# Four stacked graph layers on one core: the last normalisation and the squares for the lengths on ScalarE, its bias on GpSimd, and a new order of the steady part

## The chip, the cores and the metric

The kernel runs on one core of one Trainium2 chip. The time is the device time in microseconds (us), lower is better; it is the median of several runs of the same program. TensorE is called PE here, VectorE DVE, ScalarE ACT, GpSimd POOL and SyncE SP, as in the profile.

## The reference

The input is `x` (16 graphs, 1024 nodes, 128 features, f32) and an adjacency `adj` (16 x 1024 x 1024, int32, about 3% ones). Four graph layers follow one another, each with a residual and a layer normalisation:

```python
x = _layernorm(x + _L0_gnn_ref(x, adj, W, a))          # one-head attention, leaky relu scores
x = _layernorm(x + _L1_gnn_ref(x, adj, adj, W, a))     # eight heads, elu
x = _layernorm(x + _L2_gnn_ref(x, adj, ...))           # mean of neighbours, affine norm, relu
x = _layernorm(x + _L3_gnn_ref(x, adj, W))             # four heads of 32
# _L3: Wh = x @ W[h];  scores = Wh Wh^T / sqrt(32);  softmax over neighbours;  attn @ Wh
# _layernorm: (x - mean) / sqrt(var + 1e-5)
```

The softmax of layer 3 is taken with a shift for each head: the largest squared length of a row of `Wh` (by Cauchy-Schwarz no score is above it). So the kernel needs the squares of `Wh`, their sums over 32 columns, and the maximum over all nodes.

## The kernel before

The 16 graphs go through a software pipeline of periods. A period works at the same time on graph n = f+1 (layer 0 and the start of layer 1), graph f (the 64 products of layer 1, as 32 pairs "unit1", and the start of layer 2), graph k = f-1 (layer 2 and layer 3: 32 score tiles of 128 x 1024 whose exponentials ACT makes) and graph m = f-2 (the end of layer 3: turned back, divided, residual, normalised, stored). The nodes lie in T = 8 tiles of 128 partitions.

For each engine a table (`ON_PE`, `ON_ACT`, `ON_DVE`, `ON_POOL`, `ON_SP`) gives each job its place in the order of the engine's instructions; the number is only a rank within the engine and no time. Engines meet only through semaphores. Stage 3 of the tables is the steady part, used for 13 periods (f = 2 to 14); stages 0 to 2 are the start and stage 4 is the end (f = 15, 16, 17).

Layer 3 of graph k runs so: DVE writes `x3` (`layer2_norm`, job "norm3"); PE turns it (`layer3_turn`, L825); ACT copies it to `xbT`; PE multiplies with the weights in both directions (`layer3_project`: L1020 with the nodes on partitions, then L1026 with the features on partitions); ACT copies the first result to `w3` (`layer3_project` on ACT, signal `w3_ready`) and the second to `shared` (`layer3_wide`, `wT_ready`); SP copies halves of it across partitions (`spread_far`, L713, "far"). DVE squares `w3` (L1700), sums (L1702), takes the maximum (L1704); PE and DVE spread it over the partitions (L1031, L1709, L1711, L1035, L1716), which gives `shift_ready`. The first scores (L1056, L1063, job "scores3" 0) wait for the copy across, for the shift and for `mask3_made`. That mask is a GpSimd transfer that adds -1 to the adjacency tile (L778). Other GpSimd transfers are the next adjacency (L792) and the residual added to `x4` (L784, "residual3"); all three are in one queue.

The last normalisation of graph m: DVE makes the statistics (job "stats3", L1395 to L1407), POOL the power -1/2 (`rstd_tail`, L757, into row 5 of `tsmall`), and DVE eight instructions `(x4 + row 0) * row 5`, one for each node tile (`layer3_normalise`, job "tail3", L1412, tile `elu`, of which `x4` is another name). SP then stores (`store_out`, L718). The squares go into `squares3`, another name of `yb`.

```python
def rstd(var_ready, rstd_ready, small, b, n):
    pool.wait_ge(var_ready.sem, var_ready.of(b, n + 1))
    pool.tensor_tensor(small[:, 5, :], small[:, 4, :], half_neg[:], ALU.pow).then_inc(rstd_ready.sem, 1)
```

Of the kernel before, what the change touches and what calls it, by code (L numbers as in the profile page):

```python
# [22 lines left out]
ALU = mybir.AluOpType  # L23
# [49 lines left out]
def graph_stack(nc, x, adj, L0_gnn_W, L0_gnn_a, L1_gnn_W, L1_gnn_a, L2_gnn_rel_weights, L2_gnn_self_w,  # L73
                L2_gnn_self_b, L2_gnn_ln_gamma, L2_gnn_ln_beta, L3_gnn_W, out):
    NB, N, D = x.shape
    T = N // P
# [46 lines left out]
    with ExitStack() as ctx:  # L123
# [282 lines left out]
        trstd_ready = signal("trstd_ready", 1)  # L406
        x3_ready = signal("x3_ready", 1)
# [37 lines left out]
        def schedule(tables, step):  # L445
# [3 lines left out]
            for stage, periods in zip(STAGE, SECTIONS):  # L449
                for s in range(STEPS):  # L450
# [30 lines left out]
            (dict(maxima1=92, maxima3=43, project0=[28, 29, 34], project1=90, project2=102, project3=41, scores3=[49,  # L481
                 53, 56, 58, 65, 70, 75, 82, 84, 86, 89, 93, 96, 100, 103, 105], self2=0, self_weights=-1, shift3=47,
                 sources1=94, spread0=48, spread1=97, sum1=[19, 24, 25, 26, 35, 36, 37, 38], sum2=[1, 2, 3, 6, 9, 12,
                 16, 17], top0=44, turn0=[10, 20], turn1=88, turn2=98, turn3=39, turn_back=32, unit0=[72, 73, 74, 77,
                 78, 79, 80, 81], unit1=[4, 5, 7, 8, 11, 13, 14, 15, 18, 21, 22, 23, 27, 30, 31, 33, 40, 42, 45, 46,
                 50, 51, 52, 55, 59, 60, 61, 62, 66, 67, 68, 69], values3=[54, 57, 63, 64, 71, 76, 83, 85, 87, 91, 95,
                 99, 101, 104, 106, 107]),),
            (dict(maxima1=-1, maxima3=42, project0=[-1, -1, -1], project1=-1, project2=73, project3=39, scores3=[45,
                 47, 53, 58, 61, 63, 65, 66, 69, 72, 76, 79, 83, 90, 92, 93], self2=0, self_weights=-1, shift3=44,
                 sources1=-1, spread0=-1, spread1=-1, sum1=[16, 19, 24, 25, 28, 31, 32, 34], sum2=[1, 2, 3, 4, 8, 10,  # L490
                 13, 15], top0=-1, turn0=[-1, -1], turn1=-1, turn2=71, turn3=35, turn_back=18, unit0=[-1, -1, -1, -1,
                 -1, -1, -1, -1], unit1=[5, 6, 7, 9, 11, 12, 14, 17, 20, 21, 22, 23, 26, 27, 29, 30, 33, 36, 37, 38,
                 40, 41, 43, 46, 48, 50, 51, 52, 55, 56, 57, 59], values3=[49, 54, 60, 62, 64, 67, 68, 70, 74, 75, 84,
# [253 lines left out]
        def _(pool):  # L747
# [1123 lines left out]
```

## Time and profile before

| | us |
|---|---|
| median of 3 runs (2472.6 to 2477.9) | 2477.36 |
| profiled execution, its own time | 2477.37 |
| span of its trace | 2475.3 |
| busy: PE, DVE, ACT, POOL | 2232.8, 2226.2, 1939.2, 227.8 |

The profiled execution is one run of the program; about 2 us of its time lie outside the span. Busy time leaves out waits; matmuls are pipelined and their ends are modelled. The steady part is most of the run: the mask transfer of L778 is issued once in a period, and from one issue to the next pass about 145 us.

### The profile page before, as it was taken

Reading aid. Unit: us, or ns where it says so; the run is one execution under the profiler, and the core shown is the slowest. Engines: PE = TensorE matmul, PEld = TensorE weight load, DVE = VectorE, ACT = ScalarE, POOL = GpSimd, SP = SyncE. Lnnn points to the kernel's source line nnn. Section 1 sums busy time; section 2 is a strip of 40 time slices with the busy share of each in tenths; the row PEclk is TensorE's granted clock in tenths of the full one; section 3 lists DMA queues with packets and bytes.
Section 4 is the critical chain, followed back from the end, with each engine's and each line's share of the span. In section 5 each row is a group of like instructions: output and inputs, shape, how many; then the busy total and the mean of one; then the engine's idle time right before and its main releaser. Section 6 shows DMA issues by size and latency. Waiting matters only on the chain.

```text
span 2475.3 us, 56568 instructions
## 1 busy us (share of the span) xinstructions
PE 2232.8 (90%) x23539; PEld 1506.0 (61%) x23629; DVE 2226.2 (90%) x4195; ACT 1939.2 (78%) x2152; POOL 227.8 (9%) x135
## 2 busy tenths in 40 slices
PE   4678999999999999999999999999999999998876
PEld 3567566575756657585665757566575765657431
DVE  3898899999999999999999999999999999999766
ACT  2758798787889878787987879798787978877634
POOL 0001010010101001010010101001010100101010
PEclk9889999999999999999999999999999999999988
DMA  6238034452614445251544526144352624504000
GB/s 132 89 93 162 11 98 84 111 96 70 112 50 123 86 104 103 70 112 44 129 86 96 111 52 126 48 121 95 84 123 44 127 54 121 95 27 85 19 18 17
DMA packets 258799, 212.10 MB, mean 86 GB/s; under 512 B 137648, under 2 KB 235056, under 8 KB 257584
## 3 DMA queue, kind: packets, MB, share of 16 engines
q1 hardware_dynamic: 191424, 135.61, 19.5%
q0 software_dynamic: 67120, 72.88, 19.2%
q8 instruction: 186, 3.05, 0.5%
q14 instruction: 69, 0.57, 0.1%
HBM read 151.78 MB, written 42.53 MB: 79 GB/s over the span
## 4 chain that ended last, share of the span: by engine, by line
PE 57%; DVE 22%; issue 10%; ACT 6%; DMA 3%; POOL 0%; SPq 0%; POOLq 0%; DVEq 0%; ACTq 0%
PE kp L1080 14%; PE kp L1063 10%; PE fp L883 9%; DVE weight L1586 8%; PE fp L954 7%; PE kp L1056 4%; ACT weight L1305 3%; DMA shared<-shared 2%; DVE bstat L1395 2%; PE kp L1004 2%; PE kp L935 2%; DVE yb L1412 2%; PE fp L832 1%; DVE yb L1662 1%; PE fp L972 1%
## 5 line engine op out<-in xcount | busy, mean ns | idle before, releaser
L1257 ACT ACTIVATE ramp<-s1row,tbig 128x1024 bf16<-128x1024 f32 x854 | 913.0, 1147 | 32.1 <-DVE weight L1586 31.1
L1305 ACT ACTIVATE weight<-kp,shift 128x1024 f32<-128x1024 f32 x480 | 510.8, 1110 | 206.7 <-PE kp L1063 190.4
L1586 DVE TENSOR_TENSOR weight<-ramp,AT 128x2048 bf16<-128x2048 bf16 x512 | 609.4, 1220 | 41.8 <-PE fp L954 30.9
L1080 PE MATMUL kp<-weight,w 128*33 128x512 f32 x1920 | 457.6, 600 | 15.7 <-DVE weight L1726 7.3
L954 PEld LDWEIGHTS fp<-vh_parts,weight 128*128 128x128 bf16 x8192 | 391.9, 98 | 100.3 <-DVE weight L1586 52.0
L954 PE MATMUL fp<-vh_parts,weight 128*128 128x102 bf16 x8192 | 425.5, 209 | 29.5 <-DVE weight L1586 22.6
L1726 DVE SCALAR_TENSOR_TENSOR weight<-AT,weight 128x1024 f32<-128x1024 bf16 x272 | 321.6, 1219 | 34.7 <-ACT weight L1305 34.4
L1063 PE MATMUL kp<-shared 32*128 32x512 f32 x1920 | 274.5, 641 | 16.3 <-ACT weight L1305 16.2
L1080 PEld LDWEIGHTS kp<-weight,w 128*33 128x33 f32 x1920 | 94.2, 110 | 310.3 <-issue 225.2
L883 PEld LDWEIGHTS fp<-features,weight 128*128 128x128 f32 x1920 | 218.8, 193 | 38.1 <-issue 37.3
L883 PE MATMUL fp<-features,weight 128*128 128x129 f32 x1920 | 224.2, 278 | 13.3 <-DVE weight L1496 12.6
L935 PE MATMUL kp<-vh_parts,AT 128*128 128x136 bf16 x3072 | 219.1, 232 | 1.6 <-ACT vh_rest L1173 1.1
L935 PEld LDWEIGHTS kp<-vh_parts,AT 128*128 128x128 bf16 x3072 | 211.8, 100 | 2.5 <-ACT vh_rest L1173 1.3
L1205 ACT ACTIVATE weight<-xfT,v0neg,v0s 128x1024 f32<-128x1024 f32 x128 | 155.4, 1245 | 46.7 <-PE fp L883 44.3
L1496 DVE SCALAR_TENSOR_TENSOR weight<-weight,v,AT 128x1024 f32<-128x1024 f32 x128 | 158.9, 1281 | 15.8 <-ACT weight L1205 12.1
L1004 PE MATMUL kp<-elu,AT 128*128 128x128 bf16 x1920 | 170.2, 220 | 0.0
L1001 PE MATMUL kp<-y_hi,AT 128*128 128x129 bf16 x960 | 166.2, 221 | 3.0 <-DVE elu L1646 3.0
L1063 PEld LDWEIGHTS kp<-shared 32*128 32x128 f32 x1920 | 76.1, 183 | 128.3 <-issue 67.9
L757 POOL TENSOR_TENSOR bsmall<-bsmall,half_neg 128x8 f32<-128x8 f32 x32 | 68.2, 2130 | 895.2 <-DVE bsmall L1407 895.2
L1004 PEld LDWEIGHTS kp<-elu,AT 128*128 128x128 bf16 x1920 | 148.7, 98 | 0.2
L1056 PE MATMUL kp<-AT,big 128*128 128x512 bf16 x390 | 107.5, 382 | 35.7 <-DMA shared<-shared 20.8
L1594 DVE TENSOR_REDUCE vh<-fp 128x272 f32<-128x816 f32 x128 | 128.1, 1001 | 6.2 <-PE fp L954 6.1
(222 smaller groups left out, 2690.4 us busy)
## 6 DMA issues: line engine op xcount, KB each, us to landing
s1row<-s_rows_dram SPq DMA_DIRECT2D x128, 512.0 KB, 4.3
adj_bf_dram<-in_adj_dram POOLq DMA_DIRECT2D x15, 2048.0 KB, 12.8
AT<-minus POOLq DMA_DIRECT2D x15, 2048.0 KB, 18.2
x<-in_x_dram SPq DMA_DIRECT2D x16, 512.0 KB, 5.0
xfT<-s_row_dram SPq DMA_DIRECT2D x16, 512.0 KB, 4.3
out_dram<-elu SPq DMA_DIRECT2D x16, 512.0 KB, 3.2
shared<-shared SPq DMA_DIRECT2D x30, 256.0 KB, 3.6
elu<-x POOLq DMA_DIRECT2D x15, 512.0 KB, 5.2
```

Of the source, the lines that this page charges most:

```text
L883: last = pe.matmul(sums0(b)[:, g, n * (D + 1):(n + 1) * (D + 1)], ring0(b)[:, jt % P0_RING, t * P:(t + 1) * P], h0[:, jt, :], start=(jt == ...
L935: last = pe.matmul(kp[:, SUM_A_BANKS[t // PER], n * H1 * C1:(n + 1) * H1 * C1].rearrange("p (h c) -> p h c", h=H1), AT[:, third, jt, t * P ...
L954: last = pe.matmul(fp[:, 1 + t // 4, col:col + 2 * PARTS * C1], edges[:, u % B_RING, t * P:(t + 1) * P], vh_parts[:, jt, h, :, :, :].rearr ...
L1001: pe.matmul(sums2(b)[:, g, col:col + D + 1], lhsT, y2_hi[:, jt, :], start=(jt == 0), stop=False, skip_group_check=True)
L1004: last = pe.matmul(sums2(b)[:, g, col:col + D], lhsT, low2(b)[:, jt, k, :], start=False, stop=(jt == T - 1 and k == 1), skip_group_check=True)
L1056: pe.matmul(score_banks(b, w)[:, x, :], big[:], AT[:, third, 2 * J + x, n * HALF:(n + 1) * HALF], start=True, stop=False, skip_group_check ...
L1063: last = pe.matmul(score_banks(b, w)[:, x, :], mine[:, jt * P:(jt + 1) * P], mine[:, n * HALF:(n + 1) * HALF], start=v in masks(b), stop=True,
L1080: last = pe.matmul(kp[side(h), 0, :], values3(b)[:, (2 * J + x) * H3 + h, :], weight3[:, w % P_RING, x * HALF:(x + 1) * HALF], start=(J == ...
L1257: act.activation(ramp[:, u % R_RING, :], s1row[:, h % S_RING, :], ACT.Relu, bias=tbig1[:, jt, h:h + 1], scale=BIG).then_inc(ramp_ready, 1)
L1305: act.activation(weight3[:, w % P_RING, :], score_banks(b, w).rearrange("p a n -> p (a n)"), ACT.Exp, bias=shifts3(b)[:, h:h + 1], scale=R ...
L1586: dve.tensor_tensor(edges[:, u % B_RING:u % B_RING + 2, :], ramp[:, u % R_RING:u % R_RING + 2, :], AT[:, third, jt:jt + 2, :], ALU.min).th ...
L1726: dve.scalar_tensor_tensor(out=mine, in0=AT[:, third, 2 * J:2 * J + 2, n * HALF:(n + 1) * HALF], scalar=1.0 if b < NB - 1 else 0.0, in1=mi ...
```

## The change

1. `layer3_normalise` moves from DVE to ACT: eight ACTIVATEs of 128 x 128 with function Identity, bias and scale each a column of `tsmall` (rows 6 and 5).
2. POOL's `rstd_tail` also multiplies row 0 (minus the mean) by row 5 into row 6 and signals `tshift_ready`, for which ACT waits.
3. The squares move from DVE to ACT: after the copy to `w3` ACT reads the same PSUM tile once more with function Square and writes `squares3`; only then comes `w3_ready`. DVE's L1700 and one wait go.
4. The tables of stages 3 and 4 have a new order on all five engines.

```diff
             def rstd_tail(b):
                 rstd(tvar_ready, trstd_ready, tsmall, b, 0)
+                pool.wait_ge(trstd_ready.sem, trstd_ready.of(b))
+                pool.tensor_tensor(tsmall[:, 6, :], tsmall[:, 0, :], tsmall[:, 5, :], ALU.mult) \
+                    .then_inc(tshift_ready.sem, 1)
...
             def layer3_project(b):
                 act.wait_ge(w3_made.sem, w3_made.of(b))
                 src = projected3(b).rearrange("p a (b o) -> p (a b) o", o=O3)
-                copy(values3(b)[:, :, 0:O3], src).then_inc(w3_ready.sem, 1)
+                copy(values3(b)[:, :, 0:O3], src)
+                act.activation(squares3, src, ACT.Square).then_inc(w3_ready.sem, 1)
...
+            def layer3_normalise(b):
+                act.wait_ge(tshift_ready.sem, tshift_ready.of(b))
+                for t in range(T):
+                    last = act.activation(x4[:, t, :], x4[:, t, :], ACT.Identity, bias=tsmall[:, 6, t:t + 1],
+                                          scale=tsmall[:, 5, t:t + 1])
+                last.then_inc(x4_ready.sem, 1)
...
-                dve.tensor_tensor(squares3, values3(b)[:, :, 0:O3], values3(b)[:, :, 0:O3], ALU.mult).then_inc(back.sem, 1)
-                dve.wait_ge(back.sem, back.step())
                 dve.tensor_reduce(q3[:], squares3, AX_X, ALU.add).then_inc(back.sem, 1)
...
-            def layer3_normalise(b):
-                dve.wait_ge(trstd_ready.sem, trstd_ready.of(b))
-                normalise(x4, x4, tsmall, x4_ready.sem)
...
         ON_POOL = [
...
-            (dict(adjacency=6, mask3=1, residual3=3, rstd0=5, rstd1=7, rstd2=0, rstd3=2, rstd_tail=4),),
+            (dict(adjacency=1, mask3=0, residual3=4, rstd0=6, rstd1=7, rstd2=2, rstd3=3, rstd_tail=5),),
```

The tables for the steady part, read as orders around the jobs that matter here (before, then after):

```
PE   turn3 etc.:  turn_back unit1[15] project0[2] sum1[4..7] turn3 unit1[16] project3 unit1[17] maxima3 top0 unit1[18] unit1[19] shift3 spread0 scores3[0]
                  project0[2] turn_back sum1[4..7] unit1[15] turn3 unit1[16] top0 project3 unit1[17] maxima3 unit1[18] unit1[19] shift3 spread0 scores3[0]
PE   first jobs:  self2 sum2[0..2] unit1[0] unit1[1]      |  sum2[0..2] self2 unit1[0] unit1[1]
DVE  middle:      out2 unit1[11] stats2 head1[2] unit1[12..14] affine2 unit1[15] relu2 unit1[16] finish3 norm3 head1[3] ... top0 unit1[19] lengths3
                  out2 unit1[11..12] stats2 head1[2] unit1[13..14] affine2 relu2 unit1[15] top0 unit1[16] norm3 finish3 head1[3] ... unit1[19] most0 lengths3
DVE  last jobs:   cut1[1] masked3[14] rest2 low2 cut1_third[0]  |  cut1[0] rest2 cut1[1] masked3[14] cut1_third[0] low2
ACT:              unit0[0..2] exp3[10] exp3[11] unit0[3..5]     |  unit0[0..2] tail3 exp3[10] exp3[11] unit0[3..5]
ACT:              exp3[22] sources1 exp3[23]                    |  exp3[22] exp3[23] sources1
POOL:             rstd2 mask3 rstd3 residual3 rstd_tail rstd0 adjacency rstd1
                  mask3 adjacency rstd2 rstd3 residual3 rstd_tail rstd0 rstd1
SP:               adjacency x ... far store_row sources[3] spread_row sources[4]
                  x adjacency ... far sources[3] sources[4] store_row spread_row
```

In stage 4, "tail3" of graph 14 was on DVE between `masked3[13]` and `masked3[14]` of graph 15; it is now on ACT behind its last exponential. "tail3" of graph 15 is the last job on DVE before, and the last on ACT after.

## Rows read from the trace of the kernel before

**Rows 1.** Busy time by engine in one steady period and in two stretches of it.

```profile
1236.00:1382.00 146.00, 138.55 (x1482) 94.09 (x1486) 137.20 (x260) 121.79 (x136) 14.57 (x9) 0.99 0.43 92
...
1217.30:1263.50 46.20, 42.91 (x652) 40.60 (x649) 45.58 (x97) 37.89 (x45) 8.34 (x4) 0.96 0.56 93
1268.00:1354.00 86.00, 83.91 (x657) 42.98 (x662) 78.78 (x147) 70.10 (x79) 5.95 (x4) 1.00 0.26 65
```

**Rows 2.** GpSimd in order of time: first and last mask issue, twelve intervals apart.

```profile
366.55 3.21 POOL L778 DMA_DIRECT2D AT<-minus  x1
...
2109.16 3.22 POOL L778 DMA_DIRECT2D AT<-minus  x1
```

**Rows 3.** Chain that ended last, in order of time, one period: start, us, what.

```profile
1217.29 0.06 DVE weight L1586
...
1267.71 0.81 PE kp L1056 x3
```

**Rows 4.** Groups of instructions by form: what leaves DVE, and GpSimd's power.

```profile
L1412 DVE TENSOR_SCALAR elu<-elu,tsmall 128x128 f32<-128x128 f32 x128 | 34.2, 341 | 1.8 <-POOL tsmall L757 1.8
L1700 DVE TENSOR_TENSOR yb<-w 128x1024 f32<-128x1024 f32 x15 | 18.3, 1223 | 2.1 <-ACT w L1173 2.1
L757 POOL TENSOR_TENSOR tsmall<-tsmall,half_neg 128x8 f32<-128x8 f32 x16 | 33.3, 2083 | 323.4 <-DVE tsmall L1407 323.4
```

**Rows 5.** Groups by form on ScalarE: copies, two column operands, the table load.

```profile
L1205 ACT ACTIVATE weight<-xfT,v0neg,v0s 128x1024 f32<-128x1024 f32 x128 | 155.4, 1245 | 46.7 <-PE fp L883 44.3 <-PE kp L883 2.3
L1173 ACT ACTIVATE features<-fp 128x384 f32<-128x384 f32 x64 | 30.0, 505 | 0.0
L1173 ACT ACTIVATE w<-kp 128x1024 f32<-128x1024 f32 x15 | 15.4, 1026 | 26.6 <-PE kp L1020 26.6
L1173 ACT ACT_TABLE_LOAD x1 | 1.3, 1283 | 0.8 <-PEq L1860 0.8
```

**Rows 6.** TensorE in order of time in one period; brackets: idle before, releaser.

```profile
1209.36 0.61 PE L982 MATMUL kp<-bias_parts,part_rows 65*128 65x512 bf16 x2
...
1233.58 0.90 PE L954 MATMUL fp<-vh_parts,weight 128*128 128x102 bf16 x16 [0.41 <-DVE weight L1586]
...
1246.37 1.22 PE L954 MATMUL fp<-vh_parts,weight 128*128 128x102 bf16 x16 [0.35 <-DVE weight L1586]
...
1263.52 0.27 PE L1031 MATMUL kp<-ident,qmax 128*4 128x128 f32 x1 [1.44 <-DVE qmax L1704]
...
1267.71 0.81 PE L1056 MATMUL kp<-AT,big 128*128 128x512 bf16 x3 [2.05 <-DVE vh L1594]
...
1302.56 1.14 PE L1063 MATMUL kp<-shared 32*128 32x512 f32 x8
...
1336.61 1.14 PE L1063 MATMUL kp<-shared 32*128 32x512 f32 x8 [0.43 <-ACT weight L1305]
```

**Rows 7.** VectorE, then ScalarE, in order of time, same period.

```profile
1208.44 1.23 DVE L1646 TENSOR_TENSOR elu<-yf,elu 128x1024 bf16<-128x1024 f32 x1 [2.02 <-ACT elu L1173]
```

```profile
1261.40 1.02 ACT L1173 ACTIVATE shared<-kp 128x1024 f32<-128x1024 f32 x1 [0.69 <-PE kp L1026]
...
1297.63 2.11 ACT L1305 ACTIVATE weight<-kp,shift 128x1024 f32<-128x1024 f32 x2
...
1316.70 2.12 ACT L1305 ACTIVATE weight<-kp,shift 128x1024 f32<-128x1024 f32 x2 [6.11 <-PE kp L1063]
```

**Rows 8.** First scores (L1056) of two other periods: the wait for the copy across.

```profile
1122.05 0.81 PE L1056 MATMUL kp<-AT,big 128*128 128x512 bf16 x3 [3.08 <-DMA shared<-shared]
...
1412.39 0.81 PE L1056 MATMUL kp<-AT,big 128*128 128x512 bf16 x3 [1.17 <-DMA shared<-shared]
```

**Rows 9.** The end of the run: ScalarE, then VectorE.

```profile
2392.68 1.02 ACT L1173 ACTIVATE s1row<-fp 128x1024 f32<-128x1024 f32 x1 [0.73 <-PE fp L1026]
```

```profile
2304.93 2.12 DVE L1412 TENSOR_SCALAR elu<-elu,tsmall 128x128 f32<-128x128 f32 x8
...
2469.51 2.14 DVE L1412 TENSOR_SCALAR elu<-elu,tsmall 128x128 f32<-128x128 f32 x8 [1.75 <-POOL tsmall L757]
```

More of the change, by code:

```diff
@@ new lines, in graph_stack @@
+                 tail3=-1, turn0=[9, 14], turn1=70, turn2=82, turn3=21, unit0=[50, 51, 52, 56, 57, 58, 60, 61],
+                 wide3=27),),
+            (dict(cut1=[84, 86], cut1_second=[90, 91], elu=63, exp3=[31, 32, 34, 35, 38, 39, 41, 42, 46, 47, 54, 55,
+                 59, 60, 64, 65, 66, 67, 69, 70, 72, 73, 75, 76, 78, 79, 83, 85, 88, 89, 92, 93], exps0=36, exps1=80,
+                 first2=87, out3=[49, 68, 81, 97], prepare0=48, project0=[16, 17, 20], project1=74, project3=26,
+                 ramps=[0, 1, -1, 2, 3, 4, -1, 5, 6, 8, 9, 10, 11, 14, 18, 19, 21, 22, 28, -1, 29, 30, -1, 33, 37, -1,
+                 40, 43, 44, 45], ramps_ahead=[95, 96], second2=94, self2=7, sources1=77, sum1=[15, 23, 25], tail3=53,
+                 turn0=[12, 13], turn1=71, turn2=82, turn3=24, unit0=[50, 51, 52, 56, 57, 58, 61, 62], wide3=27),),
@@ L615, in graph_stack @@
             (dict(adjacency=3, mask3=0, residual3=-1, rstd0=4, rstd1=5, rstd2=1, rstd3=2, rstd_tail=-1),),
[L616 to L617 removed]
+            (dict(adjacency=1, mask3=0, residual3=4, rstd0=6, rstd1=7, rstd2=2, rstd3=3, rstd_tail=5),),
+            (dict(adjacency=-1, mask3=0, residual3=3, rstd0=-1, rstd1=5, rstd2=1, rstd3=2, rstd_tail=4),
                  dict(adjacency=-1, mask3=-1, residual3=8, rstd0=-1, rstd1=-1, rstd2=6, rstd3=7, rstd_tail=9),
@@ L627, in graph_stack @@
                  store_row=8, store_sources=10, x=0),),
-            (dict(adjacency=0, far=5, out=10, sources=[2, 3, 4, 7, 9], sources_ahead=[12, 13, 14], spread_row=8,
-                 store_row=6, store_sources=11, x=1),),
-            (dict(adjacency=-1, far=4, out=6, sources=[0, 1, 2, 3, 5], sources_ahead=[-1, -1, -1], spread_row=-1,
+            (dict(adjacency=1, far=5, out=10, sources=[2, 3, 4, 6, 7], sources_ahead=[12, 13, 14], spread_row=9,
+                 store_row=8, store_sources=11, x=0),),
+            (dict(adjacency=-1, far=5, out=6, sources=[0, 1, 2, 3, 4], sources_ahead=[-1, -1, -1], spread_row=-1,
                  store_row=-1, store_sources=-1, x=-1), dict(adjacency=-1, far=7, out=8, sources=[-1, -1, -1, -1, -1],
@@ L1342, in step @@
                         layer3_out(k, g)
+                if m is not None and s == at["tail3"]:
+                    layer3_normalise(m)
                 for w in range(U3):
@@ L1802, in step @@
                     layer2_norm(k)
-                if m is not None and s == at["tail3"]:
-                    layer3_normalise(m)
                 if k is not None and s == at["lengths3"]:
```

165 lines of the change are left out of this document (80 added, 85 removed).

## The prediction

> **What bounds the kernel now.** I read first the busy time by stretches [rows 1]. In a steady window of 146.0 us PE works 138.55 and DVE 137.20: both are at 94 to 95%, ACT is at 121.79, POOL at 14.57. So two engines are nearly full, and the question is which one is full where. The mask transfer tells the length of a period: (2109.16 - 366.55) / 12 = 145.2 us [rows 2]. Thirteen periods of it are 1888 us, three quarters of the run.
>
> The chain of waits then tells the place [rows 3]: from about 1217.3 it runs through DVE, up to 1267.71, where the first scores begin; from there it lies on PE for the rest of the period. The two stretches in [rows 1] say the same in busy time: in 46.2 us DVE works 45.58 and PE 42.91, in the following 86.0 us PE works 83.91 and DVE only 78.78. The reader is to see that a microsecond taken from DVE can only pay in the first third of the period, and that even there PE follows closely: it has 46.2 - 42.91 = 3.3 us to give.
>
> Where PE's gaps are, its own order of time shows [rows 6]: 0.41 and 0.35 us behind DVE's pairs, 1.44 us for the maximum of the lengths, 2.05 us before the first scores, later 0.43 us for an exponential. The gap before the first scores is put down to a DVE reduction in this period; in the two other periods shown it ended with the copy across (3.08 and 1.17 us) [rows 8]. The gaps of 1.44 and 2.05 us are not work but the latency of a chain: x3 turned, copied, projected, copied, sent across. Less DVE work doesn't shorten that.
>
> **What leaves DVE.** Eight normalising instructions and one square for each graph: 34.2 / 16 = 2.14 us and 1.22 us [rows 4], together 3.36 us in a period of 145.2. Over the run that is 54 us of busy time, and it is the most that this part could bring.
>
> **What comes to ACT.** The square reads the same PSUM tile as the copy to `w3`, 128 x 1024: 1.03 us by that copy, of which about 0.1 us overlaps the one before it [rows 5]. No ACTIVATE of 128 x 128 stands in the trace. The copies of 384 and 1024 columns (0.505 and 1.026 us) give 0.81 ns a column; the form with two column operands takes 1.245 us at 1024, so at 128 it is an estimated 1.245 - 896 x 0.00081 = 0.52 us [rows 5]. Eight of them cost 4.2 us with no overlap; if the two column operands cost nothing, 8 x (0.505 - 256 x 0.00081) = 2.4 us. Between these I take 3.3 us, near the row with the same operands, less 0.1 us of overlap for each. So ACT gets 4.2 us for the 3.36 us that DVE loses, and rises to 126 of 145. It's not the bound by sum, only by place.
>
> The Trainium skill, page "ScalarE: Activation LUTs", section "What ACT_TABLE_LOAD costs", gives 186 ns + 0.833 ns a column, 93 ns more for each column operand and 93 ns of overlap. By that the eight would be an estimated 3.2 us; the sum would be the same. The same page ("Rules for kernel authors") says to keep multiplications and additions on VectorE. In this trace the group on DVE takes 0.34 us each, against my 0.52 us, so the rule agrees with the rows on the price, and speaks against this change wherever ACT is the one that's awaited.
>
> **Place by place in the steady period.** All times are those of the period in [rows 6, 7].
>
> 1. Square before the wide copy. ACT's copy to `w3` would end at about 1260.7, the square at 1261.7, and the wide copy began at 1261.40, when PE had finished its input [rows 7]. It begins 0.2 to 0.3 us later, and so does everything on the copy across, which is what the first scores wait for: +0.2 us. The bounds are 0 and 1.0 us (the whole square in the way). The maximum of the lengths comes earlier, because 1.22 us on DVE are replaced by 0.9 on ACT, and because DVE has less to do; but that is not the last wait here, so it pays nothing.
>
> 2. Order between the layer-2 output and `x3`. DVE now writes `x3` before it finishes graph m, and pair 15 comes behind relu. `x3` can be some 1.2 us earlier. But PE turns it only after pair 15 and the eight sums, and that work is unchanged. It gains what it waited for: 0.35 us at 1246.37, since pair 15 is now long ready, and some of the 0.41 us at 1233.58, if DVE comes to the output of layer 2 a little ahead: I take 0.3. Sum -0.65 us.
>
> 3. Start of the period. PE took the bias product at 1209.36, with the sums of layer 2 behind it; now those sums are first. They need the lowest part, which DVE wrote from 1208.44 to 1209.67 behind ACT's copy [rows 6, 7]. DVE fills its 2.02 us of waiting with another job, but the part isn't ready sooner. PE waits about 0.3 us there: +0.3.
>
> 4. The normalisation on ACT. It stands before exponentials 10 and 11, which began at 1297.63 and ended near 1299.7 [rows 7]. With 3.3 us ahead of them they end at 1303.0. PE needs them for the scores at 1302.56 [rows 6]: it waits 0.4 us. Behind that ACT had 6.11 us of idle time before 1316.70 [rows 7], so the delay doesn't travel. Bounds: 0 us (the eight in 2.4 us end at 1302.1) and 1.3 us (4.2 us). POOL's multiplication (not in the trace; below the 2.1 us of its power [rows 4]) is hidden: the statistics are made tens of microseconds before ACT comes there.
>
> 5. Exponentials 22 and 23 are now neighbours; the row copy stood between them, and PE waited 0.43 us at 1336.61 [rows 6]. -0.4 us.
>
> 6. GpSimd's queue. The mask is issued ahead of the power, as soon as the sums of layer 2 are there, and the next adjacency right behind it. Both are awaited late: the mask by the first scores, the adjacency in the next period. The power for layer 2 now stands behind two issues (3.2 us for the mask [rows 2]), but DVE asks for it only after the output and the statistics, eight instructions each and a pair between, the output's alone at about the 0.34 us of such an instruction [rows 4], 2.7 us; a delay of the power would be 0.5 us at most. On SP x goes ahead of the turned adjacency, and the row's store behind two loads of sources; what they feed is behind several pairs. Zero, with rival C for the price if the cover fails.
>
> Sum: +0.2 - 0.65 + 0.3 + 0.4 - 0.4 = -0.15 us in a period, -2.0 us in thirteen.
>
> **The end.** For graph 15 ACT is idle and nothing hides a latency. PE's second half of the wide product waits for `w3_ready` in the last graph, and so ACT's copy of it at 2392.68 [rows 9] comes a square later: +1.0 us. The final normalisation was 2.14 us on DVE, the last work before the store [rows 9]; it becomes 3.3 us on ACT, behind one more POOL instruction: +1.2, and 0.1 to 2.1 us for the multiplication (a whole power as the upper bound [rows 4]), of which I take 0.3. In period 15, where PE isn't full, DVE's 2.12 us of normalising at 2304.93 [rows 9] and the square go from a chain that DVE often bounds; I take half of 3.4 us: -1.7. The end's sum is +0.8 us.
>
> Together -1.2 us, against the profiled execution's 2477.37 us; the median of the runs is 2477.36, so no correction is needed. Small gains that I can't place (DVE relieved by 3.36 us a period, with an order made for it) are more probable than small losses: I say 2475.5 us. A difference under 0.2%, 5 us, is about what a measurement of this kernel can't tell from none.
>
> **Rivals.**
>
> A, DVE's relief is worth more. For it speaks that DVE is full in the first stretch [rows 1, 3]; if PE's 0.41 and 0.35 us go and another 0.4 us of the latency chain, because `x3` is earlier and PE gets to it earlier, a period loses about 0.9 us: 13 x 0.9 = 12 us, 2466. PE's whole 3.3 us of gaps in that stretch is the limit: 13 x 3.3 = 43 us, 2434, which needs the latency to vanish. Against it: the gaps [rows 6, 8] show that most of the gap is not DVE's.
>
> B, ACT is in the way, the other side. If the square delays the copy across by its full 1.0 us and the normalisation holds PE by its upper bound of 1.3 us, less the 0.7 us of points 2, 3 and 5, a period grows by 1.6 us; with a part of it, 0.9 us, the end is 13 x 0.9 + 2 = 14 us later: 2491. It decides from the point where the eight ACTIVATEs take more than about 4 us. For it: ACT's idle time comes in one piece behind that place, 6.11 us before 1316.70 [rows 7], and not ahead of it.
>
> C, the transfers meet after all. The adjacency, 2 MB, now runs behind the mask into the time when residual and copy across go. Then the copy across lands late, as in the period with 3.08 us against the one with 1.17 [rows 8]: 1.9 us each, 13 x 1.9 = 25 us, 2500. For it: these rows. Against: the mask itself, which runs ahead of both, now starts earlier, since nothing of DVE's stands before it.
>
> D, Square isn't in the loaded table. The trace has one load, 1.28 us, for all functions used so far [rows 5]. Two loads a graph, before the wide copy and after it, put at least 2.6 us on ACT and 1.3 us on the chain: 16 x 1.3 = 21 us or more, 2498.
>
> **Chances.** My forecast, within 0.2%: 0.39. A, faster by over 0.2%: 0.38, with sizes spread from 2440 to 2472. B 0.14, C 0.06, D 0.03, together 0.23 slower. The range must leave out 2 in 10: the far part of A below 2461, and C, D and the far part of B above 2489. My forecast's own range is 2472 to 2482.
>
> **What would show it.** Right: DVE's busy time down by about 54 us, ACT's up by 60 to 70, PE's unchanged; a period of 144.8 to 145.4 us by the mask issues; PE's gap at the first scores still about 3 us in sum with the one for the maximum, and ended by the copy across; a gap near 0.4 us behind the normalisation on ACT; one table load. Wrong: a DVE group of the same sum as before; a gap at the first scores of 4 us or more (B, C); Identity instructions of 0.3 us, with no gap behind them (A).

## The result, and the profile after

The changed kernel takes 2509.96 us in the median (2507.65 to 2515.18, 4 runs), the kernel before on the same chip 2474.98 us (2472.39 to 2477.90, 4 runs): 1.0145 times the time before, 95% interval 1.0126 to 1.0164. The prediction was 2475.5 us with a range up to 2489; the forecast missed the sign and is 34.5 us off, 21 us of it beyond the end of the range.

The page of the changed kernel: busy time by engine, the chain that ended last, the group of the first scores, and two transfers with their time to landing (the last column).

```profile
span 2513.4 us, 56584 instructions
PE 2245.2 (89%) x23539; PEld 1504.7 (60%) x23629; DVE 2173.9 (86%) x4051; ACT 1996.9 (79%) x2296; POOL 245.6 (10%) x151
...
PE 55%; ACT 21%; issue 10%; DVE 9%; DMA 4%; SPq 0%; POOL 0%; ACTq 0%; DVEq 0%; POOLq 0%
...
L1063 PE MATMUL kp<-AT,big 128*128 128x512 bf16 x390 | 111.0, 394 | 51.3 <-DMA shared<-shared 40.7
...
adj_bf_dram<-in_adj_dram POOLq DMA_DIRECT2D x15, 2048.0 KB, 29.2
AT<-minus POOLq DMA_DIRECT2D x15, 2048.0 KB, 19.8
```

The same chain and the same group in the kernel before:

```profile
PE 57%; DVE 22%; issue 10%; ACT 6%; DMA 3%; POOL 0%; SPq 0%; POOLq 0%; DVEq 0%; ACTq 0%
...
L1056 PE MATMUL kp<-AT,big 128*128 128x512 bf16 x390 | 107.5, 382 | 35.7 <-DMA shared<-shared 20.8
```

What was moved has moved as intended: DVE is down by 52.3 us to 2173.9 (54 were expected) and ACT up by 57.7 to 1996.9 (60 to 70). But in the chain that ended last ACT has taken DVE's place: ACT has 21% and DVE 9%, where DVE had 22% and ACT 6%. The group with the first scores, L1063, waits 40.7 us in the run for the copy across, 20.8 us before.

In the kernel after, the groups by form that answer to [rows 4, 5]: the normalisation, the square, the table load.

```profile
L1319 ACT ACTIVATE elu<-elu,tsmall 128x128 f32<-128x128 f32 x128 | 51.0, 492 | 10.2 <-POOL tsmall L778 10.2
L1298 ACT ACTIVATE yb<-kp 128x1024 f32<-128x1024 f32 x15 | 15.3, 1018 | 0.0
L1180 ACT ACT_TABLE_LOAD x1 | 1.3, 1283 | 0.8 <-PEq L1869 0.8
```

These prices are as predicted: 0.492 us for one of the eight (0.52), 1.02 us for the square, one table load. Rival D falls. The 35 us are not in the price of an instruction.

GpSimd's mask issues, first and thirteenth, as in [rows 2]:

```profile
363.92 3.22 POOL L785 DMA_DIRECT2D AT<-minus  x1 [44.26 <-PE kp L1011]
...
2138.23 3.23 POOL L785 DMA_DIRECT2D AT<-minus  x1 [43.14 <-PE kp L1011]
```

(2138.23 - 363.92) / 12 = 147.86 us a period against 145.2: +2.64 us. The first scores of the first and the thirteenth steady period, before and then after, tell where the 38.1 us between the two spans (2513.4 - 2475.3) lie:

```profile
396.04 0.81 PE L1056 MATMUL kp<-AT,big 128*128 128x512 bf16 x3 [1.58 <-DMA shared<-shared]
...
2138.28 0.81 PE L1056 MATMUL kp<-AT,big 128*128 128x512 bf16 x3 [1.19 <-DMA shared<-shared]
```

```profile
402.26 0.81 PE L1063 MATMUL kp<-AT,big 128*128 128x512 bf16 x3 [2.27 <-DMA shared<-shared]
...
2176.37 1.37 PE L1063 MATMUL kp<-AT,big 128*128 128x512 bf16 x3 [2.27 <-DMA shared<-shared]
```

Up to the first of them the changed kernel has lost 6.2 us, in the twelve periods between them 31.9 us, and from there to the end of the span nothing: 337.0 us in both. For the start I had put nothing, for the end +0.8 us.

Windows over the stretches that answer to [rows 1], and over the first 3.7 us behind the first scores. Columns: stretch, its length, busy time and instructions of PE, its weight loads, DVE, ACT, POOL; granted clock; DMA share; GB/s.

```profile
1257.00:1403.00 146.00, 137.75 (x1449) 92.30 (x1453) 130.60 (x236) 122.50 (x142) 14.79 (x9) 0.98 0.39 88
1386.00:1432.10 46.10, 42.22 (x659) 39.58 (x657) 44.37 (x98) 37.85 (x45) 8.94 (x5) 1.00 0.76 138
1436.30:1440.00 3.70, 3.69 (x22) 1.31 (x22) 3.16 (x7) 1.43 (x3) 0.00 (x0) 0.61 0.54 192
```

The last row is what no row of the kernel before shows in this place: PE works all the time and was granted 0.61 of its clock, most of the stretch at 1.2 instead of 2.4 GHz. PE in order of time around it, the part that answers to [rows 6]:

```profile
1405.47 0.66 PE L851 MATMUL fp<-ident,x 128*128 128x128 f32 x4 [1.09 <-ACT xfT L1180]
...
1426.28 2.02 PE L1027 MATMUL kp<-rhs,xbT 128*128 128x128 f32 x16 [0.41 <-ACT vh_rest L1180]
...
1431.83 0.27 PE L1038 MATMUL kp<-ident,qmax 128*4 128x128 f32 x1 [1.08 <-DVE qmax L1719]
1431.93 1.60 PE L961 MATMUL fp<-vh_parts,weight 128*128 128x102 bf16 x32
1433.47 0.27 PE L1042 MATMUL kp<-qdiag,ones 4*128 4x4 f32 x1
...
1436.31 1.48 PE L1063 MATMUL kp<-AT,big 128*128 128x512 bf16 x3 [2.46 <-DMA shared<-shared]
1437.73 1.84 PE L1070 MATMUL kp<-shared 32*128 32x512 f32 x8
```

The three matmuls of L1063 take 1.48 us here and 0.81 in the kernel before, the eight behind them 1.84 and 1.14. In 9 of the 13 steady periods the granted clock falls like this at the scores, and the stage from the first scores to the first unit of layer 0 takes 30.7 to 31.8 us instead of 29.3. Two more periods of the changed kernel: in the first the copy across was late as well, in the second the clock stayed:

```profile
697.86 0.84 PE L1063 MATMUL kp<-AT,big 128*128 128x512 bf16 x3 [4.22 <-DMA shared<-shared]
698.63 2.09 PE L1070 MATMUL kp<-shared 32*128 32x512 f32 x8
...
993.18 0.81 PE L1063 MATMUL kp<-AT,big 128*128 128x512 bf16 x3 [2.26 <-DMA shared<-shared]
993.92 1.14 PE L1070 MATMUL kp<-shared 32*128 32x512 f32 x8
```

Read the brackets ahead of the scores with those of before. There, PE waited 1.44 us for the maximum of the lengths and 2.05 ahead of the scores [rows 6]. In six of its 13 steady periods the two waits are 1.78 and about 1.2 us [rows 8 has one of the second], in the other seven 1.43 and 1.55 to 3.08. Now the first is 1.08 in every period and the second 2.26 to 2.5 us in eight of 13, 2.67 to 4.22 in the five in which the copy across is late. Where no copy is late, the sum is 3.3 to 3.6 us against 2.9 to 3.1; the second wait has become the long one. Its length alone doesn't decide: the kernel before kept its clock behind 2.05, 2.29 and 3.08 us [rows 6, 8 have two of them], this one behind 2.26 or 2.27 us in three periods and behind 3.63 in one.

Where the period grew, in means over eleven periods of each kernel, the second to the twelfth steady one, worked out from PE's and DVE's order of time. The stages run from the reading of layer 2's sums to the turn of layer 3, its projection, the first scores, the first unit of layer 0, the projection of layer 1 that follows layer 0 (the recorded expectations call this point the layer-0 turn), and the next reading. "Half clock" counts periods in which the stage behind the scores is longer than 30.2 us.

| kernel | to turn 3 | to projection | to scores | to unit 0 | to layer 1 | to next | period | half clock |
|---|---|---|---|---|---|---|---|---|
| before | 25.67 | 2.18 | 9.86 | 29.33 | 30.98 | 47.20 | 145.23 | 0 of 11 |
| after | 25.95 | 2.58 | 10.50 | 30.52 | 31.35 | 47.11 | 148.01 | 8 of 11 |
| squares alone (e7) | 25.82 | 2.15 | 10.45 | 30.99 | 30.98 | 47.19 | 147.59 | 10 of 11 |
| squares, filled wait (e16) | 25.68 | 2.17 | 9.98 | 29.59 | 30.99 | 47.20 | 145.62 | 0 of 11 |
| normalisation alone (e8) | 25.71 | 2.17 | 9.78 | 29.36 | 31.39 | 47.19 | 145.60 | 0 of 11 |
| after, filled wait (e5) | 26.42 | 2.56 | 9.92 | 29.33 | 31.35 | 47.11 | 146.70 | 0 of 11 |
| before, filled wait (e15) | 25.68 | 2.17 | 9.56 | 29.56 | 30.99 | 47.21 | 145.17 | 0 of 11 |
| before, joined waits (e18) | 25.79 | 2.16 | 9.62 | 31.08 | 30.99 | 47.20 | 146.83 | 9 of 11 |

One caution: the first scores begin with four matmuls of 128 x 512. The traces of e15, e16 and e18 hold all four records, the others in the table only three (0.81 us, where four take 1.02). So in these three rows "to scores" is about 0.2 us too short against the others and "to unit 0" as much too long; between the two groups only the sum of these two stages can be compared. Where a record is missing, the wait in the bracket before it is too long by the same 0.2 us. It is 39.2 us before, 41.0 after, 39.1 in e15, 39.6 in e16 and 40.7 in e18.

### The profile page after: what moved, and what is told of

It reads as the page before. It is cut to its first block, busy times and chain, and to the rows that moved or that the text cites. A ratio compares the mean times of both kernels' runs of the same rounds, so it can differ in the third digit from the quotient of the medians.

```text
span 2513.4 us, 56584 instructions
## 1 busy us (share of the span) xinstructions
PE 2245.2 (89%) x23539; PEld 1504.7 (60%) x23629; DVE 2173.9 (86%) x4051; ACT 1996.9 (79%) x2296; POOL 245.6 (10%) x151
## 4 chain that ended last, share of the span: by engine, by line
PE 55%; ACT 21%; issue 10%; DVE 9%; DMA 4%; SPq 0%; POOL 0%; ACTq 0%; DVEq 0%; POOLq 0%
PE kp L1087 12%; PE kp L1070 11%; ACT ramp L1264 9%; PE fp L961 7%; PE fp L890 6%; ACT weight L1313 5%; PE kp L942 5%; PE kp L1063 4%; DVE weight L1603 4%; DMA shared<-shared 3%; ACT elu L1319 2%; PE fp L839 2%; PE fp L979 1%; PE kp L1104 1%; ACT shared L1180 1%
## 5 line engine op out<-in xcount | busy, mean ns | idle before, releaser
L961 PEld LDWEIGHTS fp<-vh_parts,weight 128*128 128x128 bf16 x8192 | 393.2, 98 | 115.9 <-issue 69.9
L961 PE MATMUL fp<-vh_parts,weight 128*128 128x102 bf16 x8192 | 424.5, 210 | 30.7 <-DVE weight L1603 15.2
L1070 PE MATMUL kp<-shared 32*128 32x512 f32 x1920 | 282.6, 658 | 17.1 <-ACT weight L1313 15.9
L942 PEld LDWEIGHTS kp<-vh_parts,AT 128*128 128x128 bf16 x3072 | 205.6, 98 | 0.7
L1063 PE MATMUL kp<-AT,big 128*128 128x512 bf16 x390 | 111.0, 394 | 51.3 <-DMA shared<-shared 40.7
L1589 DVE TENSOR_SCALAR ramp<-s1row,st 128x1024 bf16<-128x1024 f32 x170 | 120.2, 749 | 11.8 <-DMA s1row<-s_rows_dram 10.8
## 6 DMA issues: line engine op xcount, KB each, us to landing
adj_bf_dram<-in_adj_dram POOLq DMA_DIRECT2D x15, 2048.0 KB, 29.2
```

Of the source, the lines that this page charges most:

```text
L942: last = pe.matmul(kp[:, SUM_A_BANKS[t // PER], n * H1 * C1:(n + 1) * H1 * C1].rearrange("p (h c) -> p h c", h=H1), AT[:, third, jt, t * P ...
L961: last = pe.matmul(fp[:, 1 + t // 4, col:col + 2 * PARTS * C1], edges[:, u % B_RING, t * P:(t + 1) * P], vh_parts[:, jt, h, :, :, :].rearr ...
L1063: pe.matmul(score_banks(b, w)[:, x, :], big[:], AT[:, third, 2 * J + x, n * HALF:(n + 1) * HALF], start=True, stop=False, skip_group_check ...
L1070: last = pe.matmul(score_banks(b, w)[:, x, :], mine[:, jt * P:(jt + 1) * P], mine[:, n * HALF:(n + 1) * HALF], start=v in masks(b), stop=True,
```

## The experiments

Ratios are to the kernel before on the same chip. "Old order" means the order tables of the kernel before.

### Order or work: e1 to e4

e1: all that was moved, in the old order (ACT normalises behind the third unit of layer 0). e2: the kernel before with the new orders of PE, ACT, DVE, POOL and SP, nothing moved. e3: the changed kernel with the old orders of POOL and SP. e4: the changed kernel with two entries of ACT exchanged:

```
-  ... sum1[1], turn3, sum1[2], project3 ...
+  ... sum1[1], sum1[2], turn3, project3 ...
```

> All three edits of the change (normalisation and square on ACT, bias on POOL), but the orders of the kernel before; the normalisation stands behind layer-0 tile 2 on ACT, as in the changed kernel. If the new order is the cause, this is near before: 2475 plus 13 x 0.6 us (square 0.2, normalisation 0.4) plus 2 us at the end, about 2485, ratio 1.004 (range 1.000 to 1.007), steady period 145.2 to 146. If the moved work itself is the cause, it is near the changed kernel: 2510, ratio 1.014.

2514.43 us, 1.0155 (1.0140 to 1.0170). The moved work is enough by itself for a loss of this size; the new order isn't needed for it.

> The kernel before with the new orders alone; normalisation and square stay on DVE, the normalisation at its old place in the order of DVE. If the order is the cause: slower than before by 25 us or more, ratio 1.010 or above, period 147 us or more. If the moved work is the cause: within 5 us of before. An order made for a relieved DVE may do worse with the full one: up to 3.4 us a period more, 2550.

2495.35 us, 1.0078 (1.0061 to 1.0095). The new order costs with the old work, too: with DVE's work undiminished it takes 40.2 us from the projection to unit 0 instead of 39.2, and no period loses the clock at the scores.

> The changed kernel with the orders of POOL and SP of the kernel before. If the transfers that now lie close together cost the late copies across (four of twelve periods 1.2 to 1.9 us late) and the wait for row loads: 10 to 15 us less than the changed kernel, 2497, ratio 1.009. If transfers are innocent: 2510, ratio 1.014, and the half clock falls as often.

2525.01 us, 1.0202 (1.0186 to 1.0217): the new orders of GpSimd and SyncE save the changed kernel 15 us; without them the stage to turn 3 is 26.70 us instead of 25.95. Rival C named the wrong suspect: with GpSimd's old order four of the 13 copies across still land 10.7 to 11.3 us behind the projection, where a copy in time takes 9.1 to 9.4. The adjacency's 29.2 us to landing cost nothing that a run shows.

> The changed kernel with one swap on ACT in the steady part: the third sum's copy comes ahead of the copy of x3, as before. The projection no longer waits for it: 0.4 us less before the first scores in each of 13 periods, 5 us, 2505. If the shorter gap also keeps the clock up in the periods where it fell (1.5 us each, nine periods): 12 to 18 us less, 2495, ratio 1.008. If the gap simply moves to the copy across: 2510.

2506.22 us, 1.0125 (1.0110 to 1.0140), 3.7 us less, with intervals that overlap. The wait of 0.41 us at the projection is gone in the trace (2.20 instead of 2.58 us for the stage).

### Which of the two moves: e7 and e8

e7 is the kernel before with the first edit below, e8 with the second (in the old order, ACT normalises behind the third unit of layer 0).

```
 # e7: layer3_project on ACT
-                copy(values3(b)[:, :, 0:O3], src).then_inc(w3_ready.sem, 1)
+                copy(values3(b)[:, :, 0:O3], src)
+                act.activation(squares3, src, ACT.Square).then_inc(w3_ready.sem, 1)
 # and the tensor_tensor of layer3_lengths on DVE is gone
 # e8: layer3_normalise on ACT, the product of rstd_tail on POOL, as in the change
```

> The kernel before with one thing of the change: the squares by ScalarE ahead of the wide copy, no product on VectorE. Order and normalisation as before. Theory 'square': taking the product off VectorE brings the lengths' wait on PE forward and so makes of two short waits one longer one in front of the first scores, and the clock falls there: most of the old-order kernel's +38 us is already here, time 2500 to 2515. Rival 'normalisation': the square costs 0.2 us a period, 2478 to 2482, and the clock keeps its 0.97 to 0.98.

2502.92 us, 1.0105 (1.0080 to 1.0130). PE in e7, the first scores in two periods with the same wait:

```profile
546.40 1.46 PE L1056 MATMUL kp<-AT,big 128*128 128x512 bf16 x3 [2.04 <-DVE vh L1595]
...
2169.49 0.81 PE L1056 MATMUL kp<-AT,big 128*128 128x512 bf16 x3 [2.04 <-DVE vh L1595]
```

The clock was lost in the first and kept in the second; e7 loses it in 11 of 13 steady periods, also behind 1.97 us, where the kernel before kept it behind 2.05.

> The kernel before with the other half: the last normalisation as eight ACTIVATEs on ScalarE behind the third copy of the shared layer-0 turn (and the bias product on GpSimd), the product of squares still on VectorE, order otherwise as before. Theory 'square': the clock is kept, the eight cost PE 0.3 to 0.4 us a period in waits for exps and VectorE has 2.4 us more room: 2476 to 2485. Rival 'normalisation': the exps and copies of the layers behind it slip and the clock falls from that: 2500 to 2515 here.

2482.85 us, 1.0033 (1.0016 to 1.0050). The squares, the smaller of the two moves (1.2 us of DVE's time), cost 27 us; the normalisation costs 7. Together 34, while both at once in the same order cost 38 (e1) and the whole change 35. The table says where: with the squares alone 10 of 11 periods lose the clock, with the normalisation alone none, and there only the stage with the eight ACTIVATEs has grown, by 0.41 us.

### The wait ahead of the scores: e5, e6, e16, e15, e18

e5 puts matmuls of no use into PE's wait for the copy across; their product goes to a part of PSUM that nobody reads. e16 is the same on e7, e15 with eight of them on the kernel before.

```
 def layer3_spread_maxima(b):
     ...
+    if b < NB - 1:
+        for _ in range(16):
+            pe.matmul(kp[:, 4, HALF // 2:HALF], big[:], minus[:], start=True, stop=True, ...)
```

> The changed kernel with sixteen matmuls of no use (256 columns each, about 1.7 us in all) put on PE right behind the transposed maxima, in the wait for the copy across; the output doesn't change. Theory 'clock': in nine of twelve periods of the changed kernel the granted clock falls to half at the first scores, right behind PE's longest wait, and these scores and the 1.5 us around them then cost 1.4 to 1.6 us more. With PE busy in that wait the clock stays up: first scores to the first unit0 back at 29.4 us in nearly all periods, mean granted clock above 0.98, time 2496 (2490 to 2502), 12 to 20 us below the changed kernel. Rival 'ScalarE in the way': the clock only mirrors waits that cost anyway; the time stays at 2510 (2506 to 2514), whatever the clock does. Rival 'late transfer' (the copy across lands late): also unchanged, or up by at most 1 us a period if the matmuls outlast the wait.

2494.25 us, 1.0078 (1.0054 to 1.0102): 15.7 us less than the changed kernel, for work of no use. PE in order of time in e5:

```profile
1419.50 1.92 PE L1046 MATMUL kp<-minus,big 128*128 128x256 bf16 x16
1421.35 0.38 PE L872 MATMUL fp<-tmost,ones 1*128 1x1 f32 x2
1421.89 0.81 PE L1067 MATMUL kp<-AT,big 128*128 128x512 bf16 x3 [0.16 <-issue]
1422.63 1.14 PE L1074 MATMUL kp<-shared 32*128 32x512 f32 x8
```

The scores are back at 0.81 and 1.14 us, in every period, and only one of the 13 copies across is late, by 0.35 us, against five in the changed kernel. Part of the gain is lost again: the half clock now falls ahead of the turn of layer 3 in 5 of 13 periods instead of 1 (26.42 us to turn 3 instead of 25.95). The page "TensorE: Matmul & The Clock Gate" of the Trainium skill, section "HAM oscillation — how this bites in real kernels", says that a wait for a transfer between groups of matmuls can take the clock away so that the next group starts at half speed. The trace agrees, with 1.48 against 0.81 us, and here a wait of 2.3 to 2.5 us with only short matmuls ahead of it was enough in most periods.

e6 moves the square behind the wide copy in all graphs but the last.

> The changed kernel with the Square behind the wide copy instead of ahead of it, in all graphs but the last. Theory 'clock': the copy across is issued about 1.0 us earlier, but the lengths come that much later, so the wait before the transposed maxima grows and the one before the scores shrinks by as much; the clock is kept in more periods if the length of the single wait decides. Time 2500 to 2510. If only the 0.2 to 0.4 us that the Square puts ahead of the copy matter: 2507 (2504 to 2510). If the lengths set the end of that chain: the wait moves on and the time stays within 2 us of 2510.

2500.34 us, 1.0099 (1.0076 to 1.0122). The long wait is now the one for the maximum (2.81 us), the one ahead of the scores only 0.56; the scores run at full clock in all periods, but in every second one the half clock falls into the short work between the two waits (the 32 matmuls of L961 take 2.82 us instead of 1.60), and the scores come 1.3 to 1.4 us later. That is 60% of e5's gain, by moving the wait and not filling it; about 0.1 us a period of it comes from the copy across, which is issued 4.83 instead of 4.94 us behind the projection.

> Control: the kernel before with eight matmuls of no use (about 1.0 us) in the same wait. No clock is lost at its first scores, so by the theory there is nothing to win: 2476 (2473 to 2479). If such matmuls help in another way (a warmer engine later on), it becomes faster by 5 us or more, and the repair of the changed kernel proves less than I took from it.

2473.80 us, 0.9983 (0.9973 to 0.9992). Not the nothing that I expected, but 4 us and not 16: the steady part gives almost nothing (39.1 instead of 39.2 us from the projection to unit 0, a period of 145.17 instead of 145.23). Of the 5.5 us between the two profiled executions 1.5 lie ahead of the first unit 0 of the steady part and 3.6 behind the last one; why is open.

> The kernel with the squares alone on ScalarE (2503, 27.5 us over the kernel before) with the sixteen matmuls in PE's wait. Theory 'clock': the scores run at the full clock again (first scores to unit0 29.33 us in all periods) and the late copies across go as they did in the changed kernel: 2479 (2476 to 2484). Rival: if 10 us or more of the 27.5 stay, the moved squares cost something besides: 2488 or more.

2482.11 us, 1.0020 (1.0011 to 1.0029): of the squares' loss 21 us are gone (1.0105 to 1.0020). What is left is 0.4 us a period. Against e15, which has a filler and no moved square, 0.42 us more lie in the stage to the scores; 0.13 of it are late copies (two against one), so at most about 0.3 is left for the square ahead of the wide copy, which was priced at 0.2; e16's filler is also the longer one.

e18 is the converse: the kernel before, nothing moved to another engine, PE's order alone changed so that the work between its two waits now lies ahead of both.

```
-  ... unit1[17], maxima3, top0, unit1[18], unit1[19], shift3, spread0, scores3[0] ...
+  ... unit1[17], unit1[18], unit1[19], maxima3, top0, shift3, spread0, scores3[0] ...
```

> The kernel before with PE's order alone changed: the two units of layer 1 that stand between the transposed maxima and their spread (1.60 us) now ahead of the transposed maxima. PE's wait there (1.43 to 1.78 us) is filled, and what idles comes in one piece of about 3 us right ahead of the first scores, with nothing but short matmuls in it. Theory 'shape of the wait': the granted clock falls at the first scores as in the changed kernel, in half of the periods or more, 1.5 us each, and some of the copies land late: 2488 to 2500. Rival 'the moved work': the clock is kept, and the order costs the 0.2 us by which the maxima turn later: 2476 to 2480.

2499.01 us, 1.0087 (1.0073 to 1.0100). PE in order of time, and the granted clock of two stretches of e18:

```profile
1569.94 0.27 PE L988 MATMUL kp<-ident,qmax 128*4 128x128 f32 x1
...
1570.83 0.38 PE L992 MATMUL kp<-qdiag,ones 4*128 4x4 f32 x2 [0.51 <-DVE qdiag L1668]
1571.34 0.38 PE L822 MATMUL fp<-tmost,ones 1*128 1x1 f32 x2
1573.92 1.87 PE L1013 MATMUL kp<-AT,big 128*128 128x512 bf16 x4 [2.21 <-DMA shared<-shared]
1575.72 2.09 PE L1020 MATMUL kp<-shared 32*128 32x512 f32 x8
```

```profile
1573.90:1580.00 6.10, 6.08 (x39) 3.20 (x40) 6.00 (x20) 3.27 (x5) 1.52 (x1) 0.50 0.66 216
1580.00:1600.00 20.00, 20.00 (x197) 9.10 (x194) 15.11 (x25) 18.85 (x21) 0.59 (x1) 1.00 0.09 27
```

The scores begin no later than before (9.62 against 9.86 us behind the projection, of which 0.2 is the missing record), and the kernel is 22 us slower: 40.7 instead of 39.2 us from the projection to unit 0. So the same loss comes without any of the change's work, from where PE's idle time lies. In this period the scores come 4.0 us behind the start of the transposed maxima, and in that time PE has only six short matmuls. The last wait is not longer than it was: mostly 1.6 to 2.2 us, and the clock was lost behind one of 1.63 too.

### The place of the normalisation: e9, e13

Both are e8 with `tail3` later in ACT's order: e9 behind `unit0[7]`, in the 6.12 us in which ACT waits, e13 behind `exp3[13]`.

> The kernel with the normalisation alone on ScalarE (old order, squares on VectorE), the eight ACTIVATEs now behind the eighth unit of layer 0, where ScalarE waits 6.12 us for PE, instead of behind the third. Theory 'ScalarE in PE's way': the 0.43 us a period that PE waits between the first unit of layer 0 and the layer-0 turn is all that the moved normalisation cost; it goes: 2477 (2473 to 2480), equal to the kernel before. Rival 'relief': VectorE's 2.1 us less are worth something when nothing is paid for them: 2466 to 2472. Rival 'other cost' (store of the output later, GpSimd's product): stays at 2483.

2531.06 us, 1.0218 (1.0202 to 1.0234). DVE in e9:

```profile
1338.82 1.22 DVE L1487 TENSOR_TENSOR yf<-vh_rest,rec 128x1024 f32<-128x1024 f32 x1
1343.43 0.69 DVE L1492 TENSOR_SCALAR elu<-yf 128x1024 f32<-128x1024 f32 x1 [3.38 <-DMA out_dram<-elu]
```

The output's buffer is written again by layer 1's elu; DVE waits for the store out of it, 3.38 us. The idle slot had a deadline behind it, on another engine.

> The normalisation alone on ScalarE, now behind the fourteenth exp, ahead of the seventh unit of layer 0: 1.65 us of its 3.2 lie in a wait of ScalarE there, and it ends some 4.5 us before VectorE writes the buffer again. Theory 'place': PE's 80 matmuls of layer 0 (9.2 us) cover the rest, the store lands in time: unit0 to the layer-0 turn at 31.0 to 31.2 us, time 2478 (2474 to 2481). Rival 'store late': VectorE still waits for the store, by 0.5 to 1 us a period: 2484 to 2490. Rival 'relief': 2466 to 2472.

2485.05 us, 1.0033 (1.0020 to 1.0046): no better than e8. The store is in time, but the stage takes 31.66 us instead of 31.39. My "place" theory falls; no place that I tried is free.

### Repairs and a faster version: e10, e11, e12, e14, e17

> The kernel before with only GpSimd's and SyncE's orders of the changed kernel (mask, adjacency first; row stores behind the fifth load). In the changed kernel these orders were worth 15 us. If that holds by itself, by fewer late copies across and earlier masks: 2465 (2460 to 2470). If they only mend waits that the moved squares made: 2475 (2472 to 2478); the three of twelve periods in which the copy across is late by 0.5 to 1.6 us stay.

The kernel before with the new orders of POOL and SP: 2476.18 us, 0.9994 (0.9982 to 1.0005), nothing measurable. What they saved in e3 they save only together with the rest of the change.

> The changed kernel with three repairs at once: sixteen matmuls of no use in PE's wait for the copy across (measured alone: 15.7 us less), ScalarE's third copy of sum1 ahead of its copy of turn3 (measured alone: 4 us less), and the normalisation behind the eighth unit of layer 0 (unit0 to the layer-0 turn back from 31.33 to about 31.0, 4.5 us less). If the causes add: 2486 (2482 to 2490). What is left above 2475 is then the stretch before the turn of layer 3, where a clock lost 20 us before the scores is no longer covered by a wait for VectorE (27.1 instead of 25.8 us in every second period), and 0.2 each for the Square and the later self2. If the three overlap: 2489 to 2494.

The changed kernel with filler, e4's exchange and e9's late place: 2546.63 us, 1.0279 (1.0264 to 1.0294), spoilt by the late place.

> The normalisation alone on ScalarE, behind the eighth unit, with the changed kernel's orders of GpSimd and SyncE: whatever the two of this set give singly, added: 2466 if both help, 2476 if neither does. Meant as a version that keeps of the change what costs nothing.

e9 with the new orders of POOL and SP: 2531.05 us, 1.0217 (1.0201 to 1.0233), for the same reason.

> The changed kernel with the filler, ScalarE's third sum1 copy ahead of turn3's, and the normalisation at this middle place: filler alone gave 2494, the copy 4 us, the place 4.5 us if its theory holds: 2486 (2482 to 2490). If the copy's 0.4 us is lost again in the clock of the stretch before (27.1 us between the sums of layer 2 and the turn of layer 3 in more than every second period): 2490 to 2494.

e11 with e13's place: 2499.48 us, 1.0091 (1.0078 to 1.0104), no better than the filler alone (1.0078, the intervals overlap). The repairs don't add: the place costs its 0.36 us, and e4's exchange saves its 0.38 us at the projection without a gain in the total.

> The kernel before with the changed kernel's orders of GpSimd and SyncE and eight matmuls of no use in PE's wait: singly 0.9994 and 0.9983 of the kernel before. Added: 0.998, 2472 (2468 to 2476). The version of this study that should beat both kernels, by little.

e17 is the kernel before with the new orders of POOL and SP and eight matmuls of no use: 2469.24 us, 0.9973 (0.9963 to 0.9984). It beats both kernels, by 7 and by 41 us, and contains nothing of the moved work.

## Why the prediction was wrong

By its own steps, per period:

1. Square before the wide copy, +0.2: SP issues the copy across 4.94 instead of 4.86 us behind the projection, and where it isn't late it lands 0.2 us later (9.4 instead of 9.1 to 9.2). That part was right. The step's last sentence was the error: "The maximum of the lengths comes earlier ... but that is not the last wait here, so it pays nothing." It costs. Pulling the maximum forward took 0.35 to 0.7 us from PE's first wait and gave it to the last one, and with that the half clock came to the first scores. I added up waits as if a microsecond of PE's idle time were the same wherever it lies, and had no term for the clock at all. In the means of the table this is +1.19 us of the stage behind the scores, and most of the +0.64 ahead of them, since e5 takes 0.58 of that back. The runs put it at 15.7 us of the 35 (e5) and 21 of e7's loss (e16), and e18 makes 22 us of the same kind with none of the moved work.

2. Order between layer 2's output and `x3`, -0.65: wrong in sign. PE's waits of 0.41 and 0.35 us for DVE's pairs are gone, but it now waits 0.49 us for a DVE reduction, 1.09 us for ACT's copy of the layer-0 turn and, at the projection, 0.41 us for ACT's third copy of layer 1's sums: +0.28 and +0.40. The chain through that stretch, in order of time:

```profile
1397.55 4.36 ACT ramp L1264 x5
...
1402.75 2.19 ACT ramp L1264 x2
1404.94 0.49 ACT xfT L1180
```

I had asked who was late before and not who would be late next. There is also a clock in it: in the kernel before, half clock at 1246.80 made the 96 matmuls of L935 take 7.23 us instead of 6.45, and the turn behind them, which otherwise waited 0.90 us for DVE's `x3`, then waited for nothing. With `x3` earlier that cover is gone. The rows are of the kernel before, a period with the half clock and one without:

```profile
1246.80:1250.20 3.40, 3.40 (x31) 3.34 (x28) 3.26 (x17) 2.14 (x3) 0.06 (x1) 0.50 1.37 164
1248.38 7.23 PE L935 MATMUL kp<-vh_parts,AT 128*128 128x136 bf16 x96
...
1393.25 6.45 PE L935 MATMUL kp<-vh_parts,AT 128*128 128x136 bf16 x96
1400.60 1.09 PE L825 MATMUL kp<-ident,x 128*128 128x128 f32 x8 [0.90 <-DVE x L1412]
```

In e5 the stage to the turn takes 25.84 us with the full clock and 27.13 where the half clock falls into it.

3. Start of the period, +0.3: 21.31 instead of 21.13 us from layer 2's lowest part to the sums read. Right.

4. The normalisation on ACT, +0.4: the eight take 3.19 us, and the stage is 0.37 us longer; alone, in e8, 0.41. Right in mechanism and size, also against the 3.2 us that the Trainium skill's page "ScalarE: Activation LUTs" (section "What ACT_TABLE_LOAD costs") gave as an estimate.

5. Exponentials 22 and 23, -0.4: from the projection of layer 1 to layer 2's lowest part 25.80 instead of 26.07 us, -0.27. Right, a little small.

6. GpSimd's queue, 0: e10 says nothing measurable for the kernel before; for the changed one the new order is a gain of 15 us, which I had not seen.

The end, +0.8: by the scores of the first and thirteenth steady period the end didn't grow (337.0 us in both), and the start, for which I had no term, grew by 6.2 us. No run took either apart.

Of the rivals, B (ACT in the way) is true as 2 and 4 show, with about 1.05 us a period (0.28 + 0.40 + 0.37), but its own condition, eight ACTIVATEs over 4 us, was not what decided. A is refuted: DVE's 52 us bought nothing that a run shows. C saw the sign of a gap over 3 us in the periods of [rows 8], but the cause was not GpSimd's new order: late copies are there with the old one too (e3, e7). All but one went in each of e5 and e6, where the scores keep the clock; but the kernel before and e16 keep it as well and have one that is 1.5 to 1.7 us late, so what makes them late isn't shown. What was to show the prediction wrong did so: a gap at the first scores of 4 us in some periods.

The sum of what is shown: 16 us for the clock and the late copies (e5), 7 for the normalisation (e8), 5 that the squares still cost with the wait filled (e16), 4 for ACT's exchange (e4, intervals overlap). That is 32 of 35, from kernels in two orders, so the division is rough; e14 shows that such parts don't simply add. Left open: what besides the length of the wait decides on the clock, since the kernel before kept it behind 3.08 us and e18 lost it behind 1.63; what makes the copy across late in every third period, and why the stretch before the turn loses the clock in seven of 13 in the kernel before.

## What to carry to other kernels

Where TensorE waits, write down each wait with its length and its place, and look at the granted clock of the matmuls behind it: two short waits with work between them can be free, and a stretch of waits with only short matmuls in it, ahead of dense work, cost about 1.5 us in most periods. Making something earlier that isn't awaited last is therefore not always worth nothing; it can lengthen the wait that is. And an idle slot of an engine is only free up to the next writer of the buffers that the moved work holds.

## What the runs showed of the hardware

- Three matmuls of 128 x 512 took 0.81 us at the full clock and 1.48 behind a wait of 2.46 us; the granted clock of that stretch was 0.61, in e18 0.50 (1.2 GHz) behind one of 2.21 us. In the kernel before, with 1.60 us of matmuls between its two waits, it was never lost there, not behind 3.08 us either; in the changed kernel it was kept behind 2.26 us three times and behind 3.63 once; in e18 it was lost behind 1.63.
- The same loss costs between nothing and 1.6 us by what lies behind it: nothing ahead of the turn in the kernel before, where PE otherwise waited 0.90 us; 1.3 us there in e5 (27.13 against 25.84); 1.6 at the scores (30.9 against 29.3).
- 1.92 us of useless matmuls for each graph but the last made the changed kernel 15.7 us faster.
- Square ran with the one table that was loaded, like Exp, Identity and Copy: one load of 1.28 us in the run.
